# Last node stage, second normalization, routing and scatter by tiles in one stage; expert results accumulated into x2 in memory

## The chip, the cores and the metric

The kernel runs on one core of a Trainium2 chip. The core has a matmul engine (TensorE, PE; its weight loads are PEld), a Vector engine (VectorE, DVE), ScalarE (ACT), GpSimd (POOL) and a sync engine (SyncE, SP) whose work is to issue transfers; 16 DMA engines move the data. The engines run side by side and wait for each other on semaphores. The metric is the device time in microseconds of one execution.

## The reference

A graph network layer (GPS). Nodes x (6250 x 256) are normalized, then go through a three-layer graph attention network over 200,000 edges and, beside it, a linear attention block ("mix"). Both are added to x; that sum is called x2 here. Last comes a mixture of experts on the normalized x2:

```python
xn = _layernorm(x)
x  = x + gnn(xn, edge_index, ...) + mix(xn[None], ...)[0]          # x2
x  = x + ffn(_layernorm(x)[None], ...)[0]

def ffn(x, gamma, beta, Wr, br, W1, b1, W2, b2):                    # 8 experts, 2 per token
    mu = mean(x); var = mean(square(x - mu))
    xn = (x - mu) * rsqrt(var + 1e-5) * gamma + beta                # normalized a second time
    logits = xn @ Wr + br
    top_vals, top_idx = top_k(logits, 2); w = softmax(top_vals)
    for e in range(8):
        h = gelu(xn @ W1[e] + b1[e]);  y_e = h @ W2[e] + b2[e]      # 256 -> 512 -> 256
        y = y + y_e * w_full[..., e]
```

## The kernel before

Nodes are handled in 49 tiles of 128 rows (the last has 106), all in float32. Stages follow one another; each is a `Phase` with a block of one program per engine, and at its end all engines meet. The order of the work is written out by hand: each engine runs its instructions in program order, and waits on semaphores.

Up to 7674 us: the edges are laid out, the mix block runs (`mix_keys` also clears the 105 x 128 rows of `xslot` in memory from the sync queue, line 1538), and three times an edge stage (`edge_phase`, GpSimd gathers the rows of the edges' sources, line 962) and a node stage (`node_phase`). The part that this text is about is the rest:

- `node_phase(3)`, the last node stage. The sync queue loads x, rows, h and mix of a tile (lines 529 to 535), four tiles in a ring. The Vector engine interleaves two chains, `gather_in` of tile b+1 (lines 627 to 641) and `finish` of tile b (lines 651 to 679): attention result, layer norm, two residuals; the result `Hn` is x2. GpSimd stores it (line 558).
- `move_tiles("load_x2")` reads all of x2 back into `XF` in one transfer (line 1433); `normalize_tiles("norm_ffn", twice=True)` normalizes twice, two passes of 49 instructions and statistics (lines 1377 to 1404).
- `route`: GpSimd copies a tile to a stage, the matmul engine transposes it (line 1494), ScalarE copies it out of the accumulators (line 2050), a product with `Wr` gives the 8 logits (line 2031). When all tiles are there, the Vector engine finds the two best experts of all tokens (lines 2069 and 2073), the matmul engine ranks tokens within experts (lines 2039 and 2040), and the slot of each token is worked out. Only then GpSimd scatters the rows of `XF` to their slots in `xslot`, 98 indirect transfers (line 2006). The experts' weights are loaded meanwhile.
- `experts`: 105 tiles of slots, each of one expert. A tile is loaded (line 2174), transposed (2200), multiplied by W1 (2207), biased by the Vector engine (2287), put through gelu by ScalarE (2267), transposed (2215), copied (2294), multiplied by W2 (2222), biased (2301) and stored to `yslot` (2183).
- `combine`: x2 is loaded once more, GpSimd gathers two rows of `yslot` for each token (line 2336, 98 transfers), the Vector engine multiplies them by their weights and adds them to x2 (line 2348), and the sync queue stores the output (line 2357).

## Time and profile before

| | us |
|---|---|
| median of 3 runs | 8846.11 (8845.78 to 8846.94) |
| profiled execution | 8845.85 |
| its span | 8844.2 |
| busy in the span: PE / DVE / ACT / POOL | 4967.0 / 5742.0 / 1214.2 / 5339.9 |
| last node stage starts | 7674.4 |
| x2 is reloaded | 7872.6 |
| second normalization starts | 7894.3 |
| routing starts | 7956.3 |
| first load of the experts | 8183.56 |
| x2 is loaded for the combine | 8695.03 |

Times in a view are microseconds from the start of the span, unless ns is said. Busy time of an engine leaves out register, branch, semaphore and DMA-issuing instructions. "Idle before" is the time in which the engine stood still ahead of these instructions, with what ended it; "issue" is idle time in which it waited for nothing that the profile shows. The clock is the granted clock of the matmul engine as a share of 2.4 GHz. For a transfer, a timeline row on SPq or POOL is the issuing, not the moving of data.

### The profile page before, as it was taken

To read this page: it belongs to the slowest core of one execution; us is meant where nothing else is said; L and a number is where in the kernel's file an instruction comes from. 1 tells how busy PE (TensorE), PEld (TensorE's weight loads), DVE (VectorE), ACT (ScalarE), POOL (GpSimd) and SP (SyncE) were. 2 spreads that over 40 slices of the span, in tenths; PEclk is the share of its full clock that TensorE was granted. 3 is DMA by queue.
4 is the path that set the end of the run, shared out by engine and by line. 5 is a ranking of instruction groups with operands and counts; after the bars stand their busy time and mean duration, and the time that the engine had idled before them with its cause. 6 is when DMAs were issued, how large, how long until landed. Compare 5 with 4: busy or idle time off the path is not lost. (4 is left out here: it accounts for less than half of the span.)

```text
span 8844.2 us, 126083 instructions
## 1 busy us (share of the span) xinstructions
PE 4967.0 (56%) x21027; PEld 3641.5 (41%) x21028; DVE 5742.0 (65%) x14940; ACT 1214.2 (14%) x4944; POOL 5339.9 (60%) x5881
## 2 busy tenths in 40 slices
PE   1853566666666646656566665456565666402992
PEld 1542444444444424444444443344444444302561
DVE  3564676677767766776677678577777776781333
ACT  0322111111111111111111102111111111000220
POOL 1104777777777367777777762777777777405114
PEclk6976777777777667777777775677777777755996
DMA  3004444444444244444444433444444444443114
GB/s 111 21 3 155 136 135 135 132 135 135 135 132 135 85 121 132 135 135 135 132 135 135 135 111 120 131 135 135 135 134 133 136 135 135 116 127 109 56 56 129
DMA packets 477331, 1065.17 MB, mean 120 GB/s; under 512 B 133014, under 2 KB 259620, under 8 KB 475180
## 3 DMA queue, kind: packets, MB, share of 16 engines
q0 software_dynamic: 271728, 750.68, 30.6%
q1 hardware_dynamic: 205164, 310.67, 10.6%
q14 instruction: 412, 3.38, 0.1%
q8 instruction: 27, 0.44, 0.0%
HBM read 960.74 MB, written 102.53 MB: 120 GB/s over the span
## 5 line engine op out<-in xcount | busy, mean ns | idle before, releaser
L962 POOL DMA_INDIRECT edges_G<-rows,edges_index x4980 | 4765.0, 957 | 1547.1 <-issue 1492.4
L1070 PE MATMUL edges_ps_o<-edges_G,edges_OH 128*128 128x264 f32 x9960 | 3462.8, 517 | 392.1 <-DVE acc L1248 373.2
L1070 PEld LDWEIGHTS edges_ps_o<-edges_G,edges_OH 128*128 128x128 f32 x9960 | 2516.0, 263 | 1134.4 <-DVE acc L1248 528.7
L1230 DVE TENSOR_TENSOR edges_G<-edges_G,edges_ps_w 128x1024 f32<-128x1024 f32 x1245 | 1502.9, 1207 | 0.0
L1248 DVE TENSOR_TENSOR acc<-acc,edges_ps_o 128x264 f32 x2490 | 1054.1, 423 | 278.6 <-DVE acc L1248 165.0
L1129 DVE TENSOR_TENSOR edges_tu<-edges_ad,edges_G 128x80 f32<-128x80 f32 x249 | 74.9, 301 | 1448.4 <-DMA edges_G<-rows,edges_index 1448.4
L1222 DVE TENSOR_TENSOR edges_OH<-edges_ps_iota,relT 128x512 f32<-128x512 f32 x1245 | 848.1, 681 | 1.3
L1045 PE MATMUL edges_ps_s<-ident,edges_greatest 128*128 128x128 f32 x249 | 115.7, 465 | 1121.8 <-DVE edges_greatest L1190 1121.8
L989 ACT ACTIVATE edges_ps_w<-edges_diff 128x80 f32<-128x80 f32 x249 | 60.1, 241 | 4174.0 <-DVE edges_diff L1210 4174.0
L1037 PE MATMUL edges_ps_s<-ident,edges_alpha 128*128 128x128 f32 x249 | 94.2, 378 | 941.8 <-DVE edges_alpha L1134 941.8
L981 ACT ACTIVATE edges_node<-terms 128x12 bf16 x2490 | 528.5, 212 | 173.0 <-issue 96.7
L1045 PEld LDWEIGHTS edges_ps_s<-ident,edges_greatest 128*128 128x128 f32 x249 | 44.3, 178 | 1223.0 <-DVE edges_greatest L1190 1223.0
L1037 PEld LDWEIGHTS edges_ps_s<-ident,edges_alpha 128*128 128x128 f32 x249 | 38.3, 154 | 963.2 <-DVE edges_alpha L1134 754.4
L2183 POOL DMA_DIRECT2D yslot<-experts_Y x105 | 56.8, 541 | 457.8 <-DVE experts_Y L2301 457.8
L2287 DVE TENSOR_TENSOR experts_hid<-experts_psH,b 128x512 f32<-128x512 f32 x105 | 72.6, 692 | 318.7 <-PE experts_psH L2207 318.7
L1028 PE MATMUL edges_ps_s<-edges_node,edges_OHT 128*128 128x12 bf16 x4980 | 161.1, 168 | 210.8 <-DVE edges_run L1143 136.9
L1028 PEld LDWEIGHTS edges_ps_s<-edges_node,edges_OHT 128*128 128x128 bf16 x4980 | 147.0, 96 | 296.1 <-issue 198.8
L1116 DVE TENSOR_SCALAR edges_OHT<-edges_rels,lane 128x1280 bf16<-128x1280 bf16 x498 | 255.8, 555 | 0.0
L778 PE MATMUL node_psB<-node_Wx,node_hT 128*128 128x264 f32 x588 | 245.3, 563 | 0.0
L2207 PE MATMUL experts_psH<-W,experts_xs 128*128 x420 | 210.6, 624 | 32.1 <-issue 31.2
L561 POOL DMA_DIRECT2D rows<-node_ext x147 | 79.7, 542 | 243.8 <-ACT node_ext L739 125.5
L999 ACT ACTIVATE edges_fade<-edges_ps_s 128x4 f32<-128x4 f32 x249 | 43.1, 173 | 1188.4 <-DVE acc L1238 1135.7
(306 smaller groups left out, 5722.6 us busy)
## 6 DMA issues: line engine op xcount, KB each, us to landing
edges_rels<-rel SPq DMA_DIRECT2D x249, 640.0 KB
edges_G<-rows,edges_index POOLq DMA_INDIRECT x4980
edges_links<-links SPq DMA_DIRECT2D x1992, 0.1 KB
rows<-node_ext POOLq DMA_DIRECT2D x147, 130.0 KB, 2.6
node_rows<-rows SPq DMA_DIRECT2D x147, 130.0 KB, 2.1
h<-node_Hn POOLq DMA_DIRECT2D x147, 128.0 KB, 2.5
edges_masks<-lanes SPq DMA_DIRECT2D x996, 15.0 KB
experts_X<-xslot SPq DMA_DIRECT2D x105, 128.0 KB, 2.1
```

The lines of the kernel that those rows point to most:

```text
L778: mm = pe.matmul(psB[slot % 2][:, 0:RW + H], hT[:, slot % TILE_RING, k, :], Wx[:, k, :], start=(k == 0), stop=(k == 1))
L962: g.indirect_dma_start(G[n][:, s, 0:RW], None, dr["rows"], bass.IndirectOffsetOnAxis(index[n][:, s:s + 1], 0)).then_inc(gathered[n], 16)
L981: ins = a.activation(node[n][:, g, :], terms[:, bass.ds(b, 1), :, :].rearrange("p a h k -> p (a h k)"), ACT.Copy)
L1028: mm = pe.matmul(ps_ad[:, s * KEPT:(s + 1) * KEPT], OHT[:, s, :], node[n][:, s // 2, :], start=True, stop=True)
L1037: pe.transpose(ps_turn, alpha[n][:, :, :].rearrange("p h s -> p (h s)"), ident[:, :]).then_inc(turned, 1)
L1045: pe.transpose(ps_back, greatest[:, :], ident[:, :]).then_inc(turned_back, 1)
L1070: mm = pe.matmul(ps_o[g % BANKS][:, 0:GW], OH[:, 2 * g + j, :], G[n][:, 2 * g + j, :], start=(j == 0), stop=(j == 1))
L1116: v.tensor_scalar(OHT[:, s, :].rearrange("p s e -> p (s e)"), rels[:, c * WG * P:(c + 1) * WG * P], lane[:, 0:1], None, ALU.is_equal).then ...
L1222: v.tensor_tensor(OH[:, 4 * k:4 * k + 4, :], ps_iota.unsqueeze(1).broadcast_to([P, 4, P]), rel.unsqueeze(2).broadcast_to([P, 4, P]), ALU.i ...
L1230: v.tensor_tensor(g4[:, :, :, 0:D], g4[:, :, :, 0:D], ps_w[:, 4 * k:4 * k + 4, :].unsqueeze(3).broadcast_to([P, 4, H, D]), ALU.mult).then_ ...
L1248: v.tensor_tensor(a, a, ps_o[g % BANKS][:, 0:GW], ALU.add).then_inc(added, 1)
L2207: mm = pe.matmul(psH[slot % 2][:, :], xs[:, slot % 2, k * P:(k + 1) * P], W1[:, bass.ds(e, 1), k, :].rearrange("p a f -> p (a f)"), start= ...
```

## The change

`node_phase` keeps layers 0 to 2. A new function, `final_phase`, does the last node stage, the second normalization, the routing and the scatter tile by tile. Its Vector program interleaves up to four chains: `gather(b+2)`, `finish(b)`, `second(b-1)` and one instruction of the routing of a batch of seven tiles. A row in memory is now 260 words: 256 of the row, normalized without gamma and beta, then token number, best expert, the second expert's weight and the difference of the two weights. As slots are handed out before the counts of the experts are known, each expert has a region of 50 tiles in `xslot` (400 tiles, 51,200 rows), and the expert stage finds tile j through a table, `place`. These 400 tiles are cleared, with a token number beyond the nodes, during the first edge stage. ScalarE applies gamma and beta while it copies a transposed tile. In the expert stage the Vector engine works out a row's weight, ScalarE multiplies the result by it, and GpSimd adds it to x2 in memory with an accumulating indirect transfer; each waits for the one before. `combine` is gone; x2 is copied to the output, and `yslot` is gone. The expert stage loads b2 itself.

```diff
+SLOT_TILES = EX * (NB + 1)
+XW = C + 4
+CLEARED = 5
+CLEARING = SLOT_TILES // CLEARED
 def edge_phase(nc, layer, st, dr):     # sync queue, layer 0 only, once a window
+                sp.dma_start(dr["xslot"][bass.ds(w * CLEARED * P, CLEARED * P), :].rearrange("(t p) c -> p t c", p=P),
+                             blank[:, :].unsqueeze(1).broadcast_to([P, CLEARED, XW])).then_inc(slots_cleared, 16)
+def final_phase(nc, st, io, dr, ff):
+    BATCHES = NB // BATCH          # 7
+    KEEP = 2 * BATCH
+    LAG = 5
+        @block.sync
...
+            for b in range(TILE_RING):
+                load(b)
+            sp.dma_start(Wr[:, :, :], io["ffn_Wr"].rearrange("(k p) e -> p k e", p=P)).then_inc(router_in, 16)
...
+            for b in range(NB):
+                sp.wait_ge(x2_ready, b + 1)
+                sp.dma_start(dr["x2"][b * P:(b + 1) * P, :], Hn[:, b % TILE_RING, :]).then_inc(x2_out[b % TILE_RING], 16)
+                if b + TILE_RING < NB:
+                    load(b + TILE_RING)
+                if b % 4 == 3 and b // 4 < EX:
+                    load_expert(b // 4)
+        @block.gpsimd
...
+            for b in range(NB):
+                if b % BATCH == 0:
+                    g.wait_ge(slots_ready, b // BATCH + 1)
+                g.wait_ge(xhat_ready, b + 1)
+                for k in range(2):
+                    g.indirect_dma_start(dr["xslot"], bass.IndirectOffsetOnAxis(slots[0:tail(b), k, b:b + 1], 0),
+                                         XH[0:tail(b), b % KEEP, :], None).then_inc(scattered[b % KEEP], 16)
+        @block.vector
...
+            v.wait_ge(vecs_in, 48)
+            v.wait_ge(router_in, 64)
...
+                v.tensor_tensor(hn, o, mix[:, slot, :], ALU.add).then_inc(x2_ready, 1)
+                yield
+                v.wait_ge(x2_ready, b + 1)
+                c2.add(v.bn_stats(stats2[:, slot, :], hn))
+                yield
+                c2.wait()
+                v.bn_aggr(mv2[:, slot, :], stats2[:, slot, :]).then_inc(stats2_ready, 1)
...
+                while done[0] < min(NB, (q + 1) * BATCH + 3):
+                    yield
+                yield from batch(q)
...
+            for b in range(NB + 1):
+                turns = [gather(b + 2)] if b + 2 < NB else []
+                if b < NB:
+                    turns.append(finish(b))
+                if b > 0:
+                    turns.append(second(b - 1))
+                done[0] = b
+                for _ in zip_longest(*turns):
+                    next(batches, None)
...
+        @block.scalar
+            for b in range(NB + 2):
+                if b + 2 < NB:
+                    std(b + 2)
+                if 2 <= b:
+                    centre(b - 2)
+                if b < NB:
+                    std2(b)
+                if 2 <= b:
+                    spread(b - 2)
+        @block.tensor
+            for b in range(NB + 1):
+                if b < NB:
+                    turn(b)
+                if b >= 1:
+                    route(b - 1)
+                if b >= BATCH + LAG - 2 and (b - LAG + 2) % BATCH == 0:
+                    rank((b - LAG + 2) // BATCH - 1)
 def experts(nc, ident, io, ff, dr, out):
+                t = sp.value_load(place[0:1, bass.ds(j, 1)], min_val=0, max_val=SLOT_TILES - 1)
+                sp.dma_start(X[:, slot, :], dr["xslot"][bass.ds(t * P, P), :]).then_inc(x_in[slot], 16)
...
+            sp.wait_ge(y_out, 16 * NT)
+            for k in range(2):
+                n = slice(k * N // 2, (k + 1) * N // 2)
+                sp.dma_start(out[n, :], dr["x2"][n, :]).then_inc(stored, 16)
...
-                g.wait_ge(y_ready2, j + 3)
-                g.dma_start(dr["yslot"][bass.ds(j * P, P), :], Y[:, slot, :]).then_inc(y_out[slot], 16)
+                wait_apart(g, y_ready, j + 1, passed_pool)
+                wait_apart(g, token_ready, j + 1, passed_pool)
+                    wait_apart(g, y_out, 16 * j, passed_pool)
+                g.indirect_dma_start(dr["x2"], bass.IndirectOffsetOnAxis(token[:, slot, :], 0), Y[:, slot, :], None,
+                                     compute_op=ALU.add).then_inc(y_out, 16)
...
+                a.wait_ge(biased2, j + 3)
+                a.wait_ge(weight_ready, j + 1)
+                    a.wait_ge(y_out, 16 * (j - TILE_RING + 1))
+                a.activation(Y[:, slot, :], Yb[:, slot % 2, :], ACT.Copy, scale=weight[:, slot, :]).then_inc(y_ready, 1)
-def combine(nc, wts, slots, dr, out):
```

Where the instructions stand now, at three places. First, the Vector engine in a step of the last node stage. Before (in the loop; `node_` names are the stage's buffers, REGISTER_ALU and ISA rows count the loop's waits and addresses), from the statistics of tile b+1 to the next step's start:

```order
L638 BN_STATS node_stats<-node_O 128x6
L675 SCALAR_TENSOR_TENSOR node_O<-node_O,node_X 128x256
L72 REGISTER_ALU
L641 BN_AGGR node_mv<-node_stats 128x2
L679 TENSOR_TENSOR node_Hn<-node_O,node_mix 128x256
L627 ISA
L627 TENSOR_TENSOR node_O<-node_rows,node_es 128x256
L651 RECIPROCAL node_rstd<-node_sd 128x1
L629 ISA
L629 TENSOR_TENSOR acc<-acc,node_es 128x4x64
L60 REGISTER_ALU
L662 SCALAR_TENSOR_TENSOR node_O<-node_O,node_mv,node_vecs 128x256
```

After (`final_` names; the step in which the first batch's choice is made):

```order
L2159 TENSOR_SCALAR final_shift<-final_mv,final_scale 128x1
L2187 TENSOR_TENSOR final_pick<-iota,final_topf 128x56
L2115 BN_AGGR final_mv<-final_stats 128x2
L2142 TENSOR_TENSOR final_Hn<-final_O,final_mix 128x256
L2195 TENSOR_TENSOR final_chosen<-final_pick 128x7x8
L2145 BN_STATS final_stats<-final_Hn 128x6
L2199 COPY final_total<-final_psR 128x8x7
L2148 BN_AGGR final_mv<-final_stats 128x2
L2101 TENSOR_TENSOR final_O<-final_rows,final_es 128x256
L2121 RECIPROCAL final_rstd<-final_sd 128x1
L2203 SCALAR_TENSOR_TENSOR final_upto<-final_go_on,final_total 128x64
L2103 TENSOR_TENSOR acc<-acc,final_es 128x4x64
```

Behind `Hn` its own statistics and their aggregate have come in, the shift of the tile before stands ahead, and routing instructions stand between (`pick`, `chosen`, `total`; `total` is read from `psR`, the result of the rank matmuls).

Second, ScalarE in the loop over the experts' tiles, before:

```order
L2259 REGISTER_ALU
L2260 ACTIVATE experts_xs<-experts_psX 128x256
L2264 REGISTER_ALU
L2266 REGISTER_ALU
L2267 ACTIVATE experts_gel<-experts_hid 128x512
L2257 REGISTER_ALU
L2260 ACTIVATE experts_xs<-experts_psX 128x256
```

and after:

```order
L2553 REGISTER_ALU
L2555 ACTIVATE experts_xs<-experts_psX,beta,gamma 128x128 x2
L2561 REGISTER_ALU
L2563 REGISTER_ALU
L2564 ACTIVATE experts_gel<-experts_hid 128x512
L2568 ISA
L2569 REGISTER_ALU
L2572 REGISTER_ALU
L2573 ACTIVATE experts_Y<-experts_Yb,experts_weight 128x256
```

The copy of x has become two halves with beta and gamma, and `Y`, the weighing of the tile before, stands behind gelu.

Third, the end of the sync queue's program, from the last turn of its loop over tiles. Before:

```order
L2159 COMPARE_AND_BRANCH
L2174 DMA experts_X<-xslot 128x256
L88 UNCONDITIONAL_BRANCH
L2351 UNCONDITIONAL_BRANCH
L2353 DMA combine_X<-x 128x49x256
L2357 DMA out<-combine_X 128x256 x48
L2357 DMA out<-combine_X 106x256
```

and after:

```order
L2441 COMPARE_AND_BRANCH
L2457 TENSOR_LOAD place
L2457 ISA x2
L2458 ISA
L2458 DMA experts_X<-xslot 128x260
L2464 DMA out<-x 64x12500 x2
L94 UNCONDITIONAL_BRANCH
```

The load of x2 and the 49 stores of the combine are replaced by two transfers from x2 (printed `x`) to the output, behind the last tile's load and a wait for all accumulations.

## Rows read from the trace of the kernel before

**Rows 1.** The table of windows. us, busy us (instructions) of each engine, clock, transfer share, GB/s
```profile
7674.00:8183.00 509.00, 58.97 (x296) 57.77 (x296) 279.97 (x1039) 37.22 (x104) 143.31 (x203) 0.50 0.40 125
7873.00:7894.00 21.00, 0.00 (x0) 0.00 (x0) 0.00 (x0) 0.00 (x0) 0.00 (x0) 0.50 0.96 306
8183.00:8695.00 512.00, 462.46 (x1890) 301.22 (x1890) 182.42 (x315) 107.61 (x211) 56.77 (x105) 0.98 0.17 54
8695.00:8844.00 149.00, 0.00 (x0) 0.00 (x0) 47.28 (x98) 0.00 (x0) 94.21 (x98) 0.50 0.56 172
```

**Rows 2.** Timeline, last node stage, Vector engine: start us, us, instruction [idle before]
```profile
7687.67 0.42 DVE L679 TENSOR_TENSOR node_Hn<-node_O,node_mix 128x256 f32<-128x256 f32 x1
...
7772.11 0.42 DVE L638 BATCH_NORM_STATS2 node_stats<-node_O 128x6 f32<-128x256 f32 x1
...
7772.44 0.41 DVE L675 SCALAR_TENSOR_TENSOR node_O<-node_O,node_X 128x256 f32<-128x256 f32 x1
...
7772.77 0.17 DVE L641 BATCH_NORM_AGGREGATE node_mv<-node_stats 128x2 f32<-128x6 f32 x1
...
7772.88 0.42 DVE L679 TENSOR_TENSOR node_Hn<-node_O,node_mix 128x256 f32<-128x256 f32 x1
...
7864.86 0.43 DVE L679 TENSOR_TENSOR node_Hn<-node_O,node_mix 128x256 f32<-128x256 f32 x1
```

**Rows 3.** Timeline, start of the last node stage
```profile
7681.41 0.43 SPq L529 DMA_DIRECT2D node_X<-in_x  x1
...
7681.87 0.43 DVE L627 TENSOR_TENSOR node_O<-node_rows,node_es 128x256 f32<-128x256 f32 x1 [0.79 <-DMA node_mix<-mix]
```

**Rows 4.** Timeline row, then groups of the routing stage: busy us, mean ns | idle before
```profile
8018.32 3.42 DVE L2069 MAX8 route_top<-route_lg 128x8 f32<-128x8 f32 x49
...
L2094 DVE TENSOR_TENSOR route_chosen<-route_pick 128x392 bf16<-128x392 f32 x1 | 2.0, 1974 | 0.0
...
L2099 DVE TENSOR_TENSOR_SCAN route_upto<-route_go_on,route_total 128x392 f32<-128x392 f32 x1 | 1.0, 974 | 0.0
```

**Rows 5.** Groups of the routing stage, matmul engine
```profile
L1494 PE MATMUL route_psA<-ident,route_stage 128*128 128x128 f32 x98 | 32.5, 438 | 289.4 <-DMA route_br<-in_L_ffn_br 289.4
```

**Rows 6.** Scatters: group, timeline; GB/s in 40 slices of 0.1 us from 8043 (first issue 8043.64)
```profile
L2006 POOL DMA_INDIRECT xslot<-XF,slots x98 | 96.4, 984 | 58.5 <-issue 29.5 <-DVE slots L2115 28.9
...
8168.02 1.56 POOL L2006 DMA_INDIRECT xslot<-XF,slots  x1 [0.30 <-issue]
...
8183.56 13.78 SPq L2174 DMA_DIRECT2D experts_X<-xslot  x7
...
GB/s 0 0 0 0 0 0 0 0 0 0 0 0 0 0 0 0 0 0 0 0 0 0 205 369 369 328 41 0 0 0 0 0 0 0 0 246 328 369 287 82
```

**Rows 7.** Groups of the expert stage, then its first and last store in the timeline
```profile
L2301 DVE TENSOR_TENSOR experts_Y<-experts_psY,b 128x256 f32<-128x256 f32 x103 | 43.7, 425 | 129.3 <-PE experts_psY L2222 129.3
...
L2260 ACT ACTIVATE experts_xs<-experts_psX 128x256 f32<-128x256 f32 x102 | 39.1, 383 | 349.4 <-PE experts_psX L2200 349.4
...
8199.42 0.61 POOL L2183 DMA_DIRECT2D yslot<-experts_Y  x1 [29.84 <-DVE experts_Y L2301]
...
8683.57 0.54 POOL L2183 DMA_DIRECT2D yslot<-experts_Y  x1 [2.44 <-DVE experts_Y L2301]
```

**Rows 8.** Chain of waits (a gather's landing), then timeline, gather and combine stage
```profile
8739.50 2.70 DMA combine_Y<-yslot,slots
...
8832.64 1.57 POOL L2336 DMA_INDIRECT combine_Y<-yslot,slots  x1 [0.30 <-issue]
...
8838.54 1.01 DVE L2348 SCALAR_TENSOR_TENSOR combine_X<-combine_Y,wts,combine_X 106x256 f32<-106x256 f32 x2 [5.24 <-DMA combine_Y<-yslot,slots]
```

**Rows 9.** Window of the first 10 us; transfers: KB each, us from issue to landing
```profile
0.00:10.00 10.00, 0.00 (x0) 0.01 (x1) 0.33 (x11) 0.02 (x1) 4.00 (x18) 1.00 0.66 241
...
dst_next<-in_dst SPq DMA_DIRECT2D x1, 781.2 KB, 7.3
```

**Rows 10.** Groups of GpSimd in the first edge stage, 900 to 2900 us
```profile
L962 POOL DMA_INDIRECT edges_G<-rows,edges_index x1586 | 1519.0, 958 | 483.1 <-issue 476.1 <-PE edges_ps_o L1070 7.0
```

More of the change, by code:

```diff
@@ L2010, in _ @@
         @block.tensor
         def _(pe):
[L2012 to L2031 removed]
+            pe.wait_ge(router_in, 64)
@@ L2251, in _ @@
         def _(a):
+            for e in range(EX):
+                a.dma_start(b2[:, e, :], broadcast_row(io["ffn_b2"][e])).then_inc(b2_in, 16)
             a.sem_inc(xs_ready2, 2)
```

802 lines of the change are left out of this document (489 added, 313 removed).

## The prediction

> **What bounds the kernel now.** I read the views in this order: the table of windows over the last 1,170 us, then the timeline and the groups of instructions in each stage, then waits and landings of the transfers. Everything ahead of 7674 us is kept except one clearing job that moves, so the sum is made from there on.
>
> The windows [rows 1] show three stretches. From 7674 to 8183 us (last node stage, reload of x2, second normalization, routing, scatter) no engine is above 280 of 509 us, and they take turns: the reload alone is 21 us at 306 GB/s with all engines idle. From 8183 to 8695 us (experts) the matmul engine is busy 462 of 512 us at a granted clock of 0.98, the 2.4 GHz level: that stage is bound by it. From 8695 to 8844 us (gather and combine) the Vector engine has 47 us of work and GpSimd 94 us: a queue of 98 indirect gathers.
>
> In the node stage the Vector engine is the bound. Its `Hn` instruction recurs at 7687.67 and 7864.86 us, 48 steps apart: 3.69 us a step, with 256-column instructions starting 0.33 us apart and the small aggregate 0.11 us before its successor [rows 2]. So a chain step that is interleaved costs its start-to-start distance, not its duration.
>
> The time of the profiled execution is 8845.85 us, 1.65 us more than its span; the median of the runs is 8846.11 us, so both can be used alike.
>
> **The change, part by part: the fused stage.** Start: the first gather step began 7.5 us after the stage's first transfer, behind the loads of tile 0 [rows 3]. Now the Vector engine waits for gamma, beta and the router too, which stand behind 3 + 16 other issues on the sync queue. At 0.43 us plus a small gap (0.46) 23 issues take 10.7 us, and a landing 2.1: first gather at 12.8 us. Two gathers then run uncovered, 2.5 us each (six links of 0.33 to 0.42 us): the first step starts near 7692 us.
>
> One step: the old twelve instructions, 3.69. The second normalization adds statistics (0.33), aggregate (0.11), a reciprocal and a shift, each as small as a MAX8: 49 of those took 3.42 us, 0.07 each, and I take 0.1 [rows 4]. That is 0.64. The statistics of `Hn` must wait for `Hn` itself with little between them (second order excerpt), and the aggregate for them: 0.42 us of duration against 0.33 of spacing, 0.2 in all. A batch of seven tiles has 36 routing instructions: 7 MAX8 at 0.07, 7 MAX_INDEX at about twice that (they issue two instructions), one permuted write of `chosen` (1.97 us for 392 elements before, so 0.3 for 56), one scan (0.97 for 392, 0.2 for 64), some twenty small ones at 0.07 to 0.15 [rows 4]; with seven waits for earlier scatters 4.5 us, 0.65 a tile. Extra waits 0.1. Sum 5.27 us a step, 258 us for 49.
>
> The batch also waits for its rank matmuls: `chosen` is followed one round later by `total`, which reads their result, and on the matmul engine they stand behind the transposes of a tile that ScalarE centres only after the aggregate of the same step. At 0.44 us for a transpose (x2, at the lower clock level of 1.2 GHz, which the windows show for the whole stage), the same for the router product (x2) and 0.4 us for each of two ScalarE instructions [rows 5] the chain is 3.2 us, of which the Vector engine covers 1.1: 2 us, six times, 12 us. Loads: a tile's four loads go out once `x2_ready` of the tile four before is set, five issues of 0.46 us and a landing of 2.8; they are wanted 5.7 us later. That just fits; after each of the eight expert loads (1.25 MB, 3 us) it does not, 1 us each, 8 us. Steps end at 7692 + 258 + 12 + 8 = 7970 us.
>
> The scatters: 98 on GpSimd at 0.98 plus 0.30 us [rows 6]. A batch needs 18 us and seven steps take 37, so five batches are hidden. `XH` holds 14 tiles; slots of batch q are cast at the end of step 7q+14, and centring tile 7q+14 needs its first scatter two steps later, so nothing stalls there. The last two batches cannot be hidden: batch 5's slots come 1 us after the last step, batch 6's some 11 us later (36 links, now without cover), within batch 5's 18 us. So 28 scatters in a row, the last one starting 1 + 27 x 1.28 + 0.6 = 36 us after 7970. From the last scatter's start to the experts' first load 15.5 us pass now [rows 6], and as many then: 8022 us. Against 8183.56 that is 162 us less. Copy to x2 moves from GpSimd to the sync queue, where it is counted above.
>
> **Experts.** From the first load to the last store 500.0 us, 104 steps of 4.66 us [rows 7]. Added on Vector: three tiny instructions a tile, 0.5 us with one wait, placed where it idles 1.26 us before the result (129.3 us over 103). If that cover were gone, it would cost at most 0.1 to 0.5 us a tile, but what waits behind it, `hT`, has 1.5 us to spare. Added on ScalarE: copy of x in two halves with scale and bias (about 0.55 for 0.38), and `weigh`, 0.4 us a tile, on an engine that is busy 107 of 512 us and idles 3.4 us before the copy. The copy ends just when `hid` is ready; a slip there would cost 0.1 us a tile. I take 0 for these. The eight broadcasts of b2 are issued by ScalarE ahead of its first copy (3.5 us, of which 2 are exposed) and the sync queue reads a tile's place first: 3 us.
>
> The new operation is the accumulating scatter. It is chained: each waits until the one before has landed. Its period is what issue to landing takes plus about 0.3 us. No row shows an accumulation. Nearest row from below: a plain scatter's packets, which run from 2.1 to 2.7 us after its issue [rows 6], and a full 128-row gather that lands 2.70 us after issue [rows 8]. From above: a slow gather (the 106-row one, 8832.64 to 8838.54, 5.9 us [rows 8]) and then as slow a write in series, 12 us. I take 3.5 us, the gather's 2.7 with another read of a packet phase (0.6) and a little: it is the row with the same shape. 3.8 us is below 4.66, so the chain is hidden, by 0.9 us only.
>
> The Trainium skill says in "Collectives: The Full Stack" (The bandwidth ceiling: the fold count and why AG ≠ RS ≠ AR) that an add in the transfer needs two source reads, both on the same ring, and so halves the rate. By that rule the packet phase would double from 0.55 to 1.1 us and the period would be near 3.6 us; no row here shows it, and the sum stays as it is.
>
> The stage then ends 8022 + 503 = 8525 us, plus 0.4 for `weigh` and 3.5 for the last scatter: 8529 us.
>
> **The end.** Gather and combine, 149 us [rows 1], go. Instead x2 is copied to the output in memory, 6.4 MB as two transfers of 64 pieces of 50 KB. In the first 10 us three such copies (2.4 MB) ran at 241 GB/s and a share of 0.66, so 365 GB/s when busy, the last landing 7.3 us after issue [rows 9]. 6.4 MB at that rate are 18 us; at the 319 GB/s of the x2 reload (306 over 0.96 [rows 1]) 20. I take 20 plus 2 to land: 8551 us; the phase's end adds 2, as it did. Bounds 18 to 35 (reading and writing memory at once).
>
> **Clearing.** 400 slot tiles of 133 KB, 53 MB, are written during the first edge stage. GpSimd is its bound: 958 ns busy and 0.3 us of issue for each gather, nothing else before it [rows 10], while the transfers' share there is below a half. So nothing is lost; before, 14 MB were cleared beside the keys, behind a 1.8 us memset: 1 to 2 us less. At the other end 53 MB are 197 us if nothing hid them.
>
> **The sum.** 162 us go in the fused stage, 4 at the experts' end (8695 − 162 = 8533 against 8529) and 125 in place of the combine (149 against 24): 291 us. The span becomes 8553 us, and with the 1.65 us outside it 8555 us, 3.3% less.
>
> **Rivals.** (A) The accumulating scatters become the bound of the expert stage. For it: they are strictly serial, and partial gathers here needed 5.9 us. Against: a full gather needs 2.7. At 5.9 + 0.3 = 6.2 us the stage is 105 x (6.2 − 4.66) = 162 us longer: 8717 us. (B) The same chain at its upper bound, 12 us: 105 x 7.4 = 777 us more, 9330 us, slower. It decides from the period at which the whole gain of 291 us is eaten: 4.66 + 291/105 = 7.4 us. (C) The fused step is longer: loads arrive late at every tile (one late mix load of 1.3 us a step) or the ScalarE and matmul chains show through. At 6.5 us a step, 49 x 1.25 = 61 us: 8616 us. For it: Vector would be the bound with four queues feeding it just in time. Against: the old stage ran 98% busy. (D) The clearing shows through in the first edge stage, since transfers there are already at 0.44: at the full 197 us, 8750 us. Against: four windows of gathers are buffered. (E) The scatter doesn't fuse as said: if the slots of a batch came so late that all 98 stood behind the last step, 70 x 1.28 = 90 us more, 8645 us; the order excludes it.
>
> **How the numbers follow.** Forecast 0.58, own range 8520 to 8600 us (step of 4.9 to 5.9 us, copy of 18 to 35). A 0.18, C 0.14, D 0.03, E 0.01, B 0.04, the rest for sums of small ones. A measurement of this kernel tells 0.2% (18 us) from no change. Faster: all but B and a tenth of A: 0.94. Slower 0.04, same 0.02. The range reaches from 8510 to 8700 us: it takes in C, E and the nearer half of A.
>
> **What would show it.** In the changed profile: `Hn` recurs every 5.1 to 5.4 us, with a wait for the rank matmuls once in seven; GpSimd scatters 28 in a row after the last `Hn`; the experts' first load lies near 8022 us; GpSimd's idle time in the expert stage ends on ScalarE's `Y`, not on its own scatter, and steps stay 4.66 us; the last 25 us are two transfers. It is wrong if GpSimd waits for its own transfer there (A, B), if Vector waits for loads (C), or if the first edge stage grows by over 10 us (D).

## The result, and the profile after

The changed kernel takes 8540.43 us (median of 4 runs, 8538.26 to 8543.02); the kernel before took 8845.94 us beside it (4 runs). The ratio is 0.9655, 95% interval 0.9638 to 0.9672. Forecast were 8555 us and a range of 8510 to 8700. The profiled execution has a span of 8541.2 us.

The table of windows of the changed kernel, with the columns of [rows 1]: the fused stage, its steps alone, the experts, the copy to the output.
```profile
7666.90:7996.60 329.70, 67.03 (x308) 61.60 (x308) 255.94 (x1136) 111.54 (x267) 107.23 (x106) 0.50 0.54 171
7684.50:7940.50 256.00, 61.70 (x284) 56.79 (x284) 229.63 (x1018) 102.76 (x252) 77.84 (x70) 0.50 0.62 195
7996.60:8518.50 521.90, 464.32 (x1890) 298.92 (x1890) 224.32 (x630) 193.97 (x421) 163.12 (x105) 0.98 0.34 55
8518.50:8541.20 22.70, 0.00 (x0) 0.00 (x0) 0.00 (x0) 0.00 (x0) 0.00 (x0) 0.50 0.84 282
```
Against [rows 1]: 509.2 us became 329.7, the experts' 511.5 became 521.9, gather and combine of 149.2 became a copy of 22.7, and everything ahead of this starts 7.5 us earlier (7674.4 to 7666.9). The sum, −179.5 + 10.4 − 126.5 − 7.5 = −303.1, is the difference of the two spans. Forecast were −162, −4, −125 and −1 to −2.

The fused stage. First the timeline rows of `Hn` in steps without routing work (as [rows 2]), then one with a late load, then what the Vector engine waited for between 7690 and 7940 us (us in total, times, longest).
```profile
7692.28 0.39 DVE L2142 TENSOR_TENSOR final_Hn<-final_O,final_mix 128x256 f32<-128x256 f32 x1
7696.70 0.39 DVE L2142 TENSOR_TENSOR final_Hn<-final_O,final_mix 128x256 f32<-128x256 f32 x1
...
7732.04 0.42 DVE L2101 TENSOR_TENSOR final_O<-final_rows,final_es 128x256 f32<-128x256 f32 x1 [1.52 <-DMA final_mix<-mix]
```
```profile
DVE final_O L2101 <- DMA final_mix<-mix: 13.3, 8, 3.7
DVE final_total L2199 <- PE final_psR L2378: 8.3, 6, 1.6
DVE final_lg L2168 <- PE final_psL L2368: 3.2, 4, 0.9
```
A step without routing is 4.42 us. Of the 256.0 us of steps 24.8 are these waits.

The tail of the stage: GpSimd's scatters, and the experts' first load (timeline; the columns are start, us, engine).
```profile
7943.90 0.96 POOL L2058 DMA_INDIRECT xslot<-final_XH,final_slots  x1 [9.70 <-DVE final_slots L2244]
...
7978.99 1.55 POOL L2058 DMA_INDIRECT xslot<-final_XH,final_slots  x1 [0.30 <-issue]
...
7996.57 3.73 SPq L2458 DMA_DIRECT2D experts_X<-xslot  x4
```
28 scatters run in a row with 0.30 us between them, as forecast; five batches lie under the steps. The last one starts 38.5 us behind the last step (36 forecast) and 17.6 us ahead of the experts' first load (15.5 forecast, [rows 6]).

The experts. First the tile `Y` and its scatter: first and last start, then what GpSimd's idle time ended on and who waited for the scatter (us, times). A wait for several semaphores is put down to the one that came last.
```profile
L2573 ACT ACTIVATE experts_Y<-experts_Yb,experts_weight x105: 507/508/511, 8015.5 to 8511.9; 128x256 f32<-128x256 f32 x105
L2476 POOL DMA_INDIRECT x<-experts_Y,experts_token x105: 1552/1552/1627, 8017.0 to 8514.7; - x105
...
  issue: 197.5, 59
  DMA x<-experts_Y,experts_token: 192.4, 95
...
  POOL x L2476: 372.6, 105
  ACT experts_Y L2573: 53.7, 50
```
105 scatters, 4.785 us apart where [rows 7] gave 4.66 for the stores; `Y` itself recurs every 4.773 us (first to last over 104), 4.656 before, so the 104 steps take 12.2 us more. The instruction takes 1.55 us; a plain one took 0.98 [rows 6]. The chain of waits at the stage's end shows its landing, and the timeline its period when nothing else holds it:
```profile
8505.64 3.72 DMA x<-experts_Y,experts_token
...
8510.13 3.82 DMA x<-experts_Y,experts_token
```
Landing 3.72 and 3.82 us after the start of the issue (3.5 forecast), the next scatter 4.49 us after the one before (3.8 forecast): behind each landing 0.77 us pass until GpSimd issues again. By this profile it looks as if the scatters had become the bound. The experiments say otherwise.

### The profile page after: what moved, and what is told of

The parts are those of the page before. It is cut to its first block and busy times, and to the rows that moved or that the text cites. A ratio compares the mean times of both kernels' runs of the same rounds, so it can differ in the third digit from the quotient of the medians.

```text
span 8541.2 us, 126708 instructions
## 1 busy us (share of the span) xinstructions
PE 4989.8 (58%) x21039; PEld 3648.4 (43%) x21040; DVE 5705.6 (67%) x15256; ACT 1375.1 (16%) x5317; POOL 5309.6 (62%) x5685
## 3 DMA queue, kind: packets, MB, share of 16 engines
q1 hardware_dynamic: 242352, 342.64, 12.6%
## 5 line engine op out<-in xcount | busy, mean ns | idle before, releaser
L2476 POOL DMA_INDIRECT x<-experts_Y,experts_token x105 | 163.1, 1554 | 372.6 <-issue 197.5
L2499 PE MATMUL experts_psH<-W,experts_xs 128*128 x420 | 210.4, 624 | 43.2 <-issue 43.0
L2058 POOL DMA_INDIRECT xslot<-final_XH,final_slots x98 | 106.3, 1084 | 206.3 <-DVE final_slots L2244 178.3
```

The source lines that it names most:

```text
L2476: g.indirect_dma_start(dr["x2"], bass.IndirectOffsetOnAxis(token[:, slot, :], 0), Y[:, slot, :], None, compute_op=ALU.add).then_inc(y_out, 16)
L2499: mm = pe.matmul(psH[slot % 2][:, :], xs[:, slot % 2, k, :], W1[:, bass.ds(e, 1), k, :].rearrange("p a f -> p (a f)"), start=(k == 0), sto ...
```

## The experiments

The first eight runs went to two chips: plain_scatter, two_sums, pe_const and combine_kept to one on which the kernel before takes 10380 us, the next four to one on which it takes 10411. The extra time lies in the edge stages: in the profiles there the last node stage, now the fused one, starts between 9198 and 9250 us (7662 to 7667 in the other profiles), in changed kernels whose code ahead of it is the same. The changed kernel itself was not run on the first of the two. So these runs are compared by the stretches behind the edge stages, which repeat to a few us (fused stage 330.5 to 335.9 us where it isn't changed; 329.7 in the result and again in after_third), and the whole time is given beside them. The last four ran where before takes 8847 us, which is the result's 8846 again.

| run | whole time, us | of before (95%) | fused | experts | `Y` to `Y` |
|---|---|---|---|---|---|
| plain_scatter | 10090 | 0.9715 (.9683 to .9747) | 330.7 | 512.2 | 4.710 |
| two_sums | 10085 | 0.9705 (.9679 to .9732) | 331.5 | 519.4 | 4.765 |
| pe_const | 10069 | 0.9694 (.9669 to .9719) | 330.5 | 504.1 | 4.518 |
| combine_kept | 10195 | 0.9819 (.9792 to .9845) | 330.6 | 520.7 | 4.710 |
| after_again | 10111 | 0.9709 (.9693 to .9726) | 334.2 | 522.8 | 4.769 |
| before_clearing | 10413 | 1.0003 (.9994 to 1.0013) | | | |
| weights_in_pieces | 10105 | 0.9703 (.9679 to .9727) | 324.9 | 522.1 | 4.776 |
| fewer_register_loads | 10108 | 0.9704 (.9688 to .9721) | 335.9 | 502.8 | 4.512 |
| pieces_and_registers | 8514.3 | 0.9625 (.9612 to .9638) | 320.9 | 503.3 | 4.523 |
| after_third | 8540.7 | 0.9654 (.9641 to .9668) | 329.7 | 521.0 | 4.776 |
| registers_two_sums | 8468.2, one run | | 330.0 | 448.1 | 4.094 |
| scatter_twice | 9001.0, one run | | 329.9 | 982.7 | 8.940 |

Fused: first transfer of the stage to the experts' first load. Experts: from there to the copy (in combine_kept to the reload of x2). `Y` to `Y`: first to last start, over 104.

**Is the chain of scatters the bound?** plain_scatter:
```diff
-                g.indirect_dma_start(dr["x2"], bass.IndirectOffsetOnAxis(token[:, slot, :], 0), Y[:, slot, :], None,
-                                     compute_op=ALU.add).then_inc(y_out, 16)
+                g.indirect_dma_start(dr["x2"], bass.IndirectOffsetOnAxis(token[:, slot, :], 0), Y[:, slot, :], None).then_inc(y_out, 16)
```


> The changed kernel with plain scatters in place of the accumulating ones in the expert stage (same indices, same wait for the scatter before; the output lacks the addition). Theory A, that the serial chain of accumulating scatters (4.5 us from one to the next when nothing else waits) is what lengthened the expert step from 4.66 to 4.78 us: with a plain scatter (about 0.97 us on GpSimd, landing 2.7 us after its issue) the chain falls to about 3.3 us, the step goes back to 4.66 to 4.68 us and the time falls by some 11 us, to 8529. Theory B, that the step is longer by the extra instructions on VectorE and ScalarE and TensorE's own gap ahead of psH: the step stays at 4.77 us and the time falls by only the last scatter's 1 us, to 8539.

two_sums:
```diff
-                if not is_zero(j):
...
-                    wait_apart(g, y_out, 16 * j, passed_pool)
-                g.indirect_dma_start(dr["x2"], bass.IndirectOffsetOnAxis(token[:, slot, :], 0), Y[:, slot, :], None,
-                                     compute_op=ALU.add).then_inc(y_out, 16)
+                if not (is_zero(i) and slot < 2):
+                    wait_apart(g, y_out[slot % 2], 16 * (2 * i + slot // 2), passed_pool)
+                g.indirect_dma_start(dr["x2b" if slot % 2 else "x2"], bass.IndirectOffsetOnAxis(token[:, slot, :], 0), Y[:, slot, :], None,
+                                     compute_op=ALU.add).then_inc(y_out[slot % 2], 16)
...
```
The waits of ScalarE, the Vector engine and the sync queue for `y_out` are split in the same way.

> The changed kernel with two sums in DRAM: tiles of even number scatter into x2, tiles of odd number into a second buffer, and a scatter waits for the one two tiles before it alone. The accumulating operation stays, its serial chain goes (the output lacks the odd tiles' part). Theory A (chain): the step goes back to 4.66 to 4.68 us, time 8529 to 8531. Theory B (extra work beside it, TensorE's gap): the step stays 4.77, time 8540. If it is the accumulation's load on the DMA queues and not its chain, plain_scatter gets faster and this one does not.

The plain scatter shortened the stage by 9 to 11 us (521.0 to 522.8 in the changed kernel's three profiles, 512.2 here): 6.6 us of it are the steps, 2.7 the shorter way from the last `Y` to the copy. But the step of two_sums should have fallen too if the chain were at fault, and it stayed: 4.765 against 4.769 to 4.776. In it GpSimd's idle time ends on `Y`, on the Vector engine or on issue, and never on a transfer. So theory A fell for the kernel as it is. Theory B does not explain plain_scatter either: that run, and combine_kept below, keep the work on the Vector engine and ScalarE and have steps of 4.71. What differs between the first two runs is the operation, not its wait.

Where the time went stands in the groups of the matmul engine (matmuls | busy us, mean ns | idle before), here before, after and in plain_scatter:
```profile
L2207 PE MATMUL experts_psH<-W,experts_xs 128*128 x420 | 210.6, 624 | 32.1 <-issue 31.2 <-ACT experts_xs L2260 0.6
```
```profile
L2499 PE MATMUL experts_psH<-W,experts_xs 128*128 x420 | 210.4, 624 | 43.2 <-issue 43.0
```
```profile
L2498 PE MATMUL experts_psH<-W,experts_xs 128*128 x420 | 210.6, 624 | 36.1 <-issue 35.6
```
Same work, and 11.1 us more of idle time ahead of `psH` in after than before: nearly all of the 12.2 us that the steps grew. In two_sums it is 41.9, in combine_kept 36.4. At this place the engine loads the number of the tile's expert into a register (L2447). The loads of the `owner` table (ns min/median/max), in the same order:
```profile
L2165 PEldq TENSOR_LOAD <-owner x210: 295/302/492, 8186.2 to 8679.2; - x105
```
```profile
L2447 PEldq TENSOR_LOAD <-owner x210: 296/304/645, 8002.0 to 8507.7; - x105
```
```profile
L2447 PEldq TENSOR_LOAD <-owner x210: 296/301/492, 9556.2 to 10054.6; - x105
```
The medians agree, the tails don't. Of the 210 loads of after 31 last over 0.4 us (mean of all 339 ns), of two_sums 22 (332 ns). In before, plain_scatter and combine_kept it is one each (303 to 304 ns), the first of all, 0.49 to 0.50 us long and ahead of the loop.

The slow ones have their place. The trace of after has 205 of the matmul engine's loads between its first and last scatter. Of the 71 that start 1.5 to 2.5 us behind a scatter's start, 36 are over 0.35 us, and of the other 134 none. The Vector engine's 206 loads show the same: 27 of 91, and none of 115. The Trainium skill says in "Perfetto Trace Analysis" (DMA Instruction — SWDGE (GPSIMD)) that the shown end of such an instruction is the end of writing its descriptors and not of the transfer; the landings at 3.72 to 3.82 us agree. The windows show when data move, here behind the scatter at 8313.87 us (columns as in [rows 1]):
```profile
8313.87:8315.87 2.00, 2.00 (x12) 1.60 (x11) 1.09 (x4) 1.32 (x3) 1.55 (x1) 1.00 0.00 0
8315.87:8317.37 1.50, 0.71 (x6) 0.47 (x5) 1.11 (x2) 0.51 (x1) 0.00 (x0) 1.00 0.85 96
```
Nothing moves for 2.0 us; over all scatters the packets run from 2.1 to 3.45 us (medians in the trace). So the slow loads are those around the transfer's start: of the 41 that start at 2.5 to 3.5 us, while packets still move, none is slow. In plain_scatter the instruction ends at 0.97 us, 0.6 us earlier, its packets run from 1.55 to 2.05 us, and no load of the matmul engine's 205 is slow, though 35 of the Vector engine's 206 are, all of them 1.25 to 1.75 us behind a scatter's start.

One such case from the timeline and the chain of waits of after: the scatter, the register load of 0.645 us, and the idle time behind the transposes, 0.79 us where the steps around it have 0.30 to 0.41.
```profile
8313.87 1.55 POOL L2476 DMA_INDIRECT x<-experts_Y,experts_token  x1 [2.99 <-DMA x<-experts_Y,experts_token]
```
```profile
L2447 PEldq TENSOR_LOAD <-owner x1: 645/645/645, 8315.9 to 8315.9; - x1
```
```profile
8311.12 0.44 PE experts_psT L2507 x4
8311.55 0.39 issue
8311.94 1.98 PE experts_psH L2499 x4
8314.14 1.73 PE experts_psY L2514 x8
8315.87 0.50 PE experts_psT L2507 x4
8316.37 0.79 issue
8317.16 1.98 PE experts_psH L2499 x4
```
Of the two loads a step, one stands between the transposes and `psH`, the other behind matmuls that still run; only the first is exposed. It takes 0.37 us on average in after and 0.30 in plain_scatter: 7.1 us over the steps, as much as the idle time fell by with the plain scatter (43.2 to 36.1). The loop handles four tiles a turn, and its four steps tell the rest. From the first transpose to the first `psH` matmul the traces give, on average:

| us | 1st | 2nd | 3rd | 4th |
|---|---|---|---|---|
| before | 1.06 | 0.92 | 0.80 | 0.84 |
| plain_scatter | 1.06 | 0.90 | 0.90 | 0.97 |
| after | 1.08 | 0.93 | 1.09 | 0.99 |

Most of what the accumulation adds is in the third step, where 22 of 26 loads are slow in after (mean of the 26: 0.50 us). What plain_scatter has more than before, 5 us in all, is in the third and fourth: there the load starts 0.08 and 0.16 us later against the first transpose than it did before, at the same length. Why it does was not settled.

That the scatter's transfer is what slows the load is read from its timing. Two runs below put the loads elsewhere in the step: in fewer_register_loads 47 of 69 inside the 1.5 to 2.5 us are slow and none of 58 outside, and in registers_two_sums, with as many accumulating scatters, none falls inside and none is slow. What in the transfer does it, no run shows.

**What do the register loads cost?** pe_const:
```diff
-                up(j + 1, slot + 1, owner_of(pe, j + 1))
+                up(j + 1, slot + 1, 0)
...
-                down(j, slot, owner_of(pe, j))
+                down(j, slot, 0)
```


> The changed kernel with TensorE taking expert 0's weights for all tiles as a constant, so that it loads no register from the owner table in the expert stage (output wrong for the other experts, same work). In the trace TensorE stands idle 0.43 us before psH in each step, put down to issue, where it was 0.33 us before the change. Theory B1, that TensorE's own register loads make this gap: the gap falls below 0.2 us and the step by up to 0.3 us, time 8505 to 8515. Theory A (chain of scatters at 4.5 us plus waits): the step can fall by no more than 0.1 us, since the chain then sets it, time 8530 to 8540.

fewer_register_loads, which computes the full result:
```diff
                 j = TILE_RING * i + slot
+                e = owner_of(pe, j) if slot == 0 else mine[0]
+                mine[0] = owner_of(pe, j + 1)
                 turn_h(j, slot)
-                up(j + 1, slot + 1, owner_of(pe, j + 1))
+                up(j + 1, slot + 1, mine[0])
...
-                down(j, slot, owner_of(pe, j))
+                down(j, slot, e)
```


> The changed kernel with TensorE's loads of the owner registers in the expert stage cut from 8 to 5 per 4 tiles (a tile's owner is kept from the step before) and both put ahead of the transposes of the GELU tile. By pe_const, which had none and took 4.52 us a step in place of 4.77, the loads cost 0.25 us a step. Theory F, that each load costs where it stands: 5 of 8 left gives 4.68, 10 us less; if the loads ahead of the transposes are covered by the psY matmuls still running, 4.55, 22 us less. Rival: TensorE's queue runs dry at the new place as at the old, within 3 us of the changed kernel.

Both took the step from 4.77 to 4.52 and 4.51, beyond the 0.1 us that theory A allowed, and fewer_register_loads did as well as having none: idle time ahead of `psH` went from 43 to 0.4 us, with 10.5 us of it now ahead of the transposes. Five of eight loads are left, so it is their place that counts: ahead of the transposes they stand beside `psY` matmuls that still run. Then the chain does bound the stage. The last `Y` starts at 10071.1 us, the last scatter at 10083.7, 12.6 us later (12.7 in pe_const); in after it was 2.8. The profiled execution is 20.0 us shorter than that of after_again, but the medians differ by 3.3 us only (0.9704 against 0.9709), on a chip where executions of the changed kernel lie up to 31 us apart.

registers_two_sums takes the chain away as well; its diff is that of the two named runs together.

> fewer_register_loads with the serial chain of scatters taken away as in two_sums (even and odd tiles to two buffers; the output lacks the odd tiles' part). In fewer_register_loads the last scatter started 12.6 us behind the last weighted tile, and scatters came every 4.62 us: theory G, that with the register loads covered it is the chain that bounds the expert stage. Then here the step falls further, to 4.35 to 4.50 us, and the last scatter follows the last weighted tile within 2 us, as in two_sums: experts 465 to 485 us from first load to copy. Rival: TensorE's matmuls bound it at the same 4.5 to 4.6; only the lag of 12 us goes: 490 us.

The step fell to 4.09 us, beyond the range of theory G, and the stage to 448.1 us. The matmul engine is its bound there, busy 425.0 of the 428 us from 8012 to 8440. In this form the chain costs 55 us, in the kernel as changed 2 to 3 (two_sums 519.4 us, the changed kernel 521.0 to 522.8): two bounds lay 0.2 us apart.

The idle time ahead of `psH`, 43 us, is less than the 71 us that the steps lost from after to here. The starts of the matmuls show the rest, in after and in registers_two_sums:
```profile
8325.62 0.60 PE L2507 MATMUL experts_psT<-ident,experts_gel 128*128 128x128 f32 x4
8326.64 1.98 PE L2499 MATMUL experts_psH<-W,experts_xs 128*128 x4 [0.41 <-issue]
8328.45 0.38 PE L2492 MATMUL experts_psX<-ident,experts_X 128*128 128x128 f32 x2
```
```profile
8200.68 0.60 PE L2507 MATMUL experts_psT<-ident,experts_gel 128*128 128x128 f32 x4
8201.12 1.88 PE L2499 MATMUL experts_psH<-W,experts_xs 128*128 x4
8202.84 0.38 PE L2492 MATMUL experts_psX<-ident,experts_X 128*128 128x128 f32 x2
```
From transposes to `psH` it is 1.02 and 0.44 us, from `psH` to `psX` 1.81 and 1.72. Averaged over all steps the two distances differ by 0.59 and 0.10 us, and that is all of the 0.68 us by which the steps differ (4.77 and 4.09). The idle row counts from the drawn end of the transposes, and 0.16 us of their 0.60 lie over the next matmul where no gap stands; behind a gap the first `psH` matmul takes 0.69 us where the others take 0.59.

scatter_twice adds a second scatter per tile behind the first:
```diff
-                    wait_apart(g, y_out, 16 * j, passed_pool)
+                    wait_apart(g, y_out, 32 * j, passed_pool)
+                g.indirect_dma_start(dr["x2"], bass.IndirectOffsetOnAxis(token[:, slot, :], 0), Y[:, slot, :], None,
+                                     compute_op=ALU.add).then_inc(y_out, 16)
+                wait_apart(g, y_out, 32 * j + 16, passed_pool)
                 g.indirect_dma_start(dr["x2"], bass.IndirectOffsetOnAxis(token[:, slot, :], 0), Y[:, slot, :], None,
                                      compute_op=ALU.add).then_inc(y_out, 16)
...
```


> The changed kernel with each tile scattered twice, the second waiting for the first (each expert result is added twice). This prices the prediction's rivals A and B: if the serial chain sets the step as soon as it is the longer one, two scatters of 4.5 us each give a step of 9.0 us and the expert stage takes 104 x (9.0 - 4.78), 440 us longer. If scatters overlap with something that the chain's 4.5 us held only once (a fixed wait for the tile), the step is 7.5 to 8.5.

Both scatters of a tile, with their durations in ns (shortest, median, longest) and the start of the first and last:
```profile
L2476 POOL DMA_INDIRECT x<-experts_Y,experts_token x105: 1543/1552/1627, 8012.6 to 8966.8; - x105
L2479 POOL DMA_INDIRECT x<-experts_Y,experts_token x105: 1544/1552/1570, 8017.3 to 8971.5; - x105
```
954.2 us for 208 periods: 4.59 us each, 9.18 us a tile, and the stage 461 us longer. The serial period is a sum that nothing hides, as rivals A and B had it, with 4.59 for their 6.2 and 12.

**What the accumulation saved.** combine_kept keeps the fused stage and undoes the second half of the change:
```diff
-                g.indirect_dma_start(dr["x2"], bass.IndirectOffsetOnAxis(token[:, slot, :], 0), Y[:, slot, :], None,
-                                     compute_op=ALU.add).then_inc(y_out, 16)
+                t = g.value_load(place[0:1, bass.ds(j, 1)], min_val=0, max_val=SLOT_TILES - 1)
+                g.dma_start(dr["xslot"][bass.ds(t * P, P), 0:C], Y[:, slot, :]).then_inc(y_out[slot], 16)
...
+        combine(nc, slots, dr, out)
```


> The changed kernel with the second part of the change undone: the expert stage writes its weighted tiles back over its own slots by plain addressed stores, and the combining stage of before reads two rows per token and adds them to x2 (two plain additions, since the weights are in the rows already; the gathered rows are 1040 bytes). What the accumulating scatters saved stands in the difference. From the traces: end 149 us as before in place of 22.7 (+126), expert step back at 4.66 if the chain of scatters had lengthened it (-11): 8655 by theory A. By theory B, where the step is longer for the work on VectorE and ScalarE that stays here: 8666.

From the start of the fused stage to the end it takes 1002.6 us where after_again, on another chip, takes 879.8: 123 us. Behind the experts' first load, where the two kernels differ, it is 672.0 against 545.5, and these 126.5 us are what the traces of before and after give for the end. The combine is 151.3 us; the expert step is 4.71, 0.06 less than after, but the stage only 2 us shorter, because the phase's end costs 10 us from the last store to the reload. The fused stage keeps its 330.6 us: the two halves of the change act apart. The fused stage itself, the larger part of the gain, was not undone in a run; its 179.5 us are read from the traces of before and after.

**The clearing.** before_clearing:
```diff
+                sp.dma_start(dr["blanks"][bass.ds(w * 5 * P, 5 * P), :].rearrange("(t p) c -> p t c", p=P),
+                             blank[:, :].unsqueeze(1).broadcast_to([P, 5, C + 4])).then_inc(slots_cleared, 16)
```


> The kernel before with the clearing of the slots added to its first edge stage exactly as the change has it (80 transfers of 650 KB from a zeroed tile, to a buffer of their own); everything else of before stays, its own clearing in the keys stage too. Theory C, that the gathers' queue waits for nothing the clearing takes: within 5 us of before (8846). Rival D of the prediction, the clearing shows through: up to 197 us more. If the 7.5 us that the changed kernel gained ahead of its last node stage came from the clearing's side effects, this kernel gains them too.

1.5 us more than before, with an interval from −6 to +14. The gathers of the first edge stage, 1000 to 3000 us, are the same in it and in after_again, which both clear; of before there is no trace from that chip:
```profile
L980 POOL DMA_INDIRECT edges_G<-rows,edges_index x1282 | 1219.7, 951 | 780.0 <-issue 366.8 <-PE edges_ps_o L1088 241.2 <-remote 171.9
```
```profile
L963 POOL DMA_INDIRECT edges_G<-rows,edges_index x1280 | 1219.1, 952 | 781.3 <-issue 363.1 <-PE edges_ps_o L1071 233.5 <-remote 184.7
```
In the profiles of the result the node stage behind the first edge stage starts at 2967.4 us before and at 2966.0 after, with the clearing. Rival D is out: 53 MB written beside the gathers cost nothing that can be measured. Nor does the clearing give the 7.5 us: they lie just outside the interval.

after_again and after_third are the changed kernel itself.

> The changed kernel itself, so that the other runs of this group have it on their own chip. Expert step 4.77 us; time 8540 us where the kernel before takes 8846, or the same share (0.9655) of another chip's time: 10020 where before takes 10380.

> The changed kernel once more, beside pieces_and_registers on the same chip: fused stage 330 to 334 us, experts 522 us, end 22.7 us.

**The late loads.** weights_in_pieces:
```diff
-                if b % 4 == 3 and b // 4 < EX:
-                    load_expert(b // 4)
+                if b < 5 * EX:
+                    load_expert(b // 5, b % 5)
```
The second number picks the piece: a half of W1, a half of W2, or b1.

> The changed kernel with the experts' weights loaded in 40 pieces (256 KB or less each, one behind each of the first 40 tiles' stores) in place of 24 larger ones (three behind every fourth tile). VectorE stood idle 13.3 us in 8 waits for the tiles' loads in the fused stage, each just behind such a group. Theory E, that the group in SP's queue makes the tile's loads late: the waits shrink to under 4 us in sum and the kernel is 8 to 12 us faster than the changed one. Rival: the weights' bytes take the same DMA time wherever they stand, the waits only spread: within 3 us.

Both edits together:

> The changed kernel with both edits that shortened a stage in the runs so far: the experts' weights in 40 pieces (fused stage 324.9 us in place of 330 to 336) and 5 register loads per 4 tiles ahead of the transposes (expert stage, first load to the copy, 502.8 us in place of 522.8). If they add up, the part from the start of the fused stage to the end takes 852 us in place of 874 to 880 and the kernel is 22 to 28 us faster than the changed one; the two act in different stages, so nothing should be lost. The edge stages ahead of it, which these edits do not touch, can hide or double this in the whole time on a chip whose runs lie 30 us apart.

The Vector engine's waits for loads of `mix` (us, times), in after_third and in pieces_and_registers:
```profile
  DVE final_O L2101: 13.3, 9
```
```profile
  DVE final_O L2105: 3.1, 7
```
10.2 of the 13.3 us come back: the fused stage takes 320.9 us in place of 329.7. In weights_in_pieces the waits are 3.2 us where after_again has 12.0, and the stage 324.9 for 334.2; its whole time is 5.7 us less, which is inside the noise there. With the register loads the kernel takes 8514.3 us, 26.4 less than the changed kernel beside it, 332 less than before. What bounds the expert stage in it stands in its chain of waits, near the end:
```profile
8467.97 3.74 DMA x<-experts_Y,experts_token
8471.75 0.51 issue
8472.25 0.04 POOLq L78
8472.29 0.04 issue
8472.35 0.08 issue
8472.48 3.80 DMA x<-experts_Y,experts_token
```
Landing 3.7 to 3.8 us, 0.5 us until GpSimd goes on, 0.2 us for its own instructions.

## Why the prediction was right, point by point

- **Start of the fused stage**: the first step begins 17.6 us after the stage's first transfer, as computed. Waits for the last router transfer show there.
- **The step** was the term mis-sized. It was set too long: 4.63 us by the terms without routing, 4.42 measured; and 0.65 a tile for the routing batches, where the average over the 48 steps from 7687.8 to 7940.2 us without those waits, (252.4 − 24.8) / 48 = 4.74, leaves 0.32. The batch of 36 small instructions cost some 2.2 us and not 4.5. Small instructions were counted at their spacing in a row of their own. Woven between wide ones they seem to cost less, which is a reading of the timeline; no run tests it. The sign "`Hn` recurs every 5.1 to 5.4 us" comes true only with the waits in it (252.4 / 48 = 5.26).
- **Stalls**: 12 for the rank and router products and 8 for loads were forecast, 11.5 and 13.3 were measured. The place was right: with the weights in pieces 3.1 of the 13.3 are left (pieces_and_registers). The six terms named for the chain of the rank matmuls (four of 0.44 us, two of 0.4) add up to 2.6 us and not to the 3.2 that were taken. Rival C's sign, the Vector engine waiting for loads, did appear, 13.3 us of it, where the sum had 8.
- **The tail**: 28 scatters, 38.5 us for 36, and the handover 17.6 for 15.5. In all the stage is 329.7 for 347.6 us: −22 in the steps, +4.6 behind them.
- **Experts, start and Vector and ScalarE work at no cost**: the first `Y` comes 18.9 us behind the first load where it was 15.1 (3.4 more forecast). That the added work costs nothing came true for the engines (Vector 224 of 522 us busy, ScalarE 194), though `xs` in two halves took 0.81 us and not 0.55.
- **"So the chain is hidden, by 0.9 us only"**: the period is 4.59 us for the 3.8 taken, since a landing took 3.7 to 3.8 us for 3.5, and what lies between it and the next issue about 0.75 us for 0.3. The cover is 0.2 us at the measured step. The conclusion held, just; two_sums shows that nothing was waiting for it. The sign given for rivals A and B, GpSimd waiting for its own transfer, did appear (95 of 105 times), so that sign was badly chosen: a wait that ends last by a little bounds nothing behind it as long as the engine behind it has slack. Two of the readings behind the 3.5 us were off. A plain scatter's packets run from 1.6 to 2.1 us behind its issue, not from 2.1 to 2.7: the slices of [rows 6] start at 8043 us, 0.64 us ahead of the issue. And the accumulation costs more than one packet phase. By the traces a plain scatter of the same rows lands after 2.42 us (plain_scatter) and an accumulating one after 3.79 (after; medians). Of these 1.37 us, 0.58 are GpSimd's longer instruction and 0.8 the packets, which run for 1.35 us in place of 0.5. The queue's account points the same way, first for 8010 to 8510 us of after, then for 9565 to 10060 of plain_scatter (packets, MB, share of 16 engines' time):
```profile
q0 software_dynamic: 14832, 13.51, 24.2%
```
```profile
q0 software_dynamic: 4992, 13.64, 7.9%
```
The Trainium skill says in "Collectives: The Full Stack" (The bandwidth ceiling: the fold count and why AG ≠ RS ≠ AR), of collectives, that an add halves the rate. Here the same bytes took 3.1 times the transfer time, in three times the packets: 1 KB each where the plain scatter moves 4 KB. So the direction agrees with that page and the size does not.
- **"Steps stay 4.66"** failed: 4.77. Missing in the forecast was that an accumulating scatter lengthens the register loads of other engines. It cost 7 of the 12.2 us; the other 5 are in the later start of the loads.
- **The end**: 22.7 us for 24. **Clearing**: no cost.
- **Luck in the sum**: the fused stage came out 18 us shorter than forecast and the expert stage 14 us longer (−4 forecast, +10.4 measured), so the whole is 15 us off where its parts are off by more.
- **Ahead of the fused stage** 7.5 us went where 1 to 2 were forecast. Where before takes 8846 us, all five profiles with the new stages start the fused stage between 7662.5 and 7666.9 us, the kernel before at 7674.4, so it is hardly chance; the gain is spread over the edge stages (the next node stages start at 2965.0 to 2966.0 for 2967.4 us, and at 5312.7 to 5315.1 for 5319.2), whose code is the same but for the clearing. Its cause was not found.

## What to carry to other kernels

Where two bounds lie close, price both before trusting the forecast step: here the matmul engine's 4.78 us hid a serial chain of 4.59, and taking 18 us off the first brought out the second, which holds back 55 us more. A wait that ends on a transfer (95 of 105 here) does not yet make the transfer the bound; taking its chain away does tell. A serial chain of transfers costs issue to landing plus the way back to the issuing engine, 0.75 us here. A register that is loaded from a table belongs ahead of a stretch in which the engine's queue is still full, and is loaded once. Load groups that share a queue with a just-in-time stream should be cut to one piece per step of that stream.

## What the runs showed of the hardware that was not expected

- A register load from on-chip memory takes 0.30 us, and up to 0.65 us on the matmul engine (0.71 on the Vector engine) when it starts 1.5 to 2.5 us behind the start of an accumulating scatter. In after 36 of 71 loads there were slow, and none of 134 elsewhere, also not those in the second half of the transfer.
- With these loads ahead of the transposes and the chain gone, the same matmuls took 4.09 us a step in place of 4.77, though the profile shows only 0.41 us a step of idle time before `psH`: a gap costs its idle time, 0.16 us by which matmuls otherwise overlap, and 0.1 us at the first matmul behind it (`psH` mean 624 ns, 598 without gaps).
- An accumulating scatter of 128 rows of 1 KB: 1.55 us on GpSimd, landing after 3.6 to 4.1 us (median 3.79), 4.59 us from one to the next in series; a plain one holds GpSimd for 0.97 us and lands after 2.42. The accumulating ones took 3.1 times the engines' transfer time for the same bytes.
- A copy of 6.4 MB inside memory in two transfers took 22.7 us, 282 GB/s at a transfer share of 0.84.
